# A two-layer adaLN kernel: its weights loaded in three groups with a semaphore each, its modulation and gate rows made inside the first image

## What is computed

```python
mod = (_silu(L0_c) @ L0_wmod).reshape(L0_c.shape[0], 6, 1, -1)
sa, ca, ga, sb, cb, gb = (mod[:, 0], mod[:, 1], mod[:, 2], mod[:, 3], mod[:, 4], mod[:, 5])
ga = (2 * (ga >= 0) - 1) * jnp.maximum(jnp.abs(ga), 0.25)
gb = (2 * (gb >= 0) - 1) * jnp.maximum(jnp.abs(gb), 0.25)
h = _layernorm(x, axis=-1) * (1 + ca) + sa
x = x + ga * _L0_attn_ref(h, ...)      # selective scan mixer
h = _layernorm(x, axis=-1) * (1 + cb) + sb
x = x + gb * _L0_ffn_ref(h, ...)       # routed experts, 8 of width 64, and a shared one
# layer 1: the same wrapping around _L1_attn_ref (gated delta rule, 8 heads)
# and _L1_ffn_ref (attention and 8 experts of width 512)
```

## Time and profile before

| | |
|---|---|
| median of 3 runs | 2970.29 us (2969.28 to 2974.66) |
| the profiled execution | 2970.33 us |
| its span | 2968.5 us |
| TensorE / VectorE / ScalarE / GpSimd busy | 82% / 74% / 41% / 22% |
| transferred | 21.39 MB: 125 GB/s in the first of 40 equal slices of the span, 1 to 8 GB/s in the others |

### The profile page before, as it was taken

One profiled execution on the slowest core, in us unless ns is written; L12 is line 12 of the kernel. 1 busy time (PEld: TensorE's weight loads), 2 busy tenths in 40 slices (PEclk: granted clock), 3 DMA queues, 4 the chain that ended last, 5 costly groups with the idle time before them and its releaser, 6 DMA issues.

```text
span 2968.5 us, 60546 instructions
## 1 busy us (share of the span) xinstructions
PE 2431.9 (82%) x22424; PEld 1916.4 (65%) x22424; DVE 2207.0 (74%) x5056; ACT 1202.5 (41%) x2697; POOL 650.6 (22%) x465
## 2 busy tenths in 40 slices
PE   1478878979887897978889887887988789798897
PEld 1166766757666585756757676675866667576685
DVE  1668777787977778787787877778697777878752
ACT  0333532435344253533525353343534425353432
POOL 0222122131212212122132212213121221312110
PEclk9569989989899998989989998998989899898999
DMA  4000000000000000000000000000000000000000
GB/s 125 2 2 3 1 7 3 7 3 7 2 3 7 3 7 3 1 8 2 8 3 7 2 3 7 3 7 3 7 2 3 7 3 7 3 3 5 1 6 2
DMA packets 24830, 21.39 MB, mean 7 GB/s; under 512 B 7217, under 2 KB 21570, under 8 KB 24530
## 3 DMA queue, kind: packets, MB, share of 16 engines
q1 hardware_dynamic: 24530, 17.26, 2.1%
HBM read 15.13 MB, written 2.13 MB: 6 GB/s over the span
## 4 chain that ended last, share of the span: by engine, by line
PE 42%; issue 27%; DVE 23%; POOL 5%; ACT 2%; SPq 1%; DMA 1%; DVEq 0%; POOLq 0%; ACTq 0%
PE banks L978 6%; PE banks L1151 4%; PE banks L1004 4%; PE banks L1141 4%; PE banks L855 4%; DVE wide L1336 3%; PE banks L970 3%; DVE wide L1324 3%; DVE wide L1344 2%; PE banks L996 2%; PE banks L918 2%; PE banks L960 2%; POOL lg L539 2%; DVE inv L1507 2%; PE banks L927 2%
## 5 line engine op out<-in xcount | busy, mean ns | idle before, releaser
L535 POOL TENSOR_TENSOR wide<-wide 128x512 f32<-128x512 f32 x128 | 260.2, 2033 | 861.0 <-DVE wide L1344 543.5
L1456 DVE SCALAR_TENSOR_TENSOR wide<-pad,conv,wide 128x256 f32<-128x256 f32 x864 | 368.6, 494 | 0.0
L637 ACT ACTIVATE wide<-small,a_neg 128x255 f32<-128x255 f32 x512 | 217.7, 496 | 188.0 <-DVE wide L1336 187.9
L1336 DVE TENSOR_TENSOR_SCAN wide<-wide 128x1024 f32<-128x1024 f32 x128 | 291.6, 2278 | 1.9 <-ACT wide L637 0.3
L762 ACT ACTIVATE inv<-banks,up1b 128x256 f32<-128x256 f32 x512 | 212.1, 489 | 126.6 <-PE banks L1141 126.4
L1141 PE MATMUL banks<-inv,up 128*128 128x256 f32 x1024 | 262.3, 387 | 0.0
L1151 PE MATMUL banks<-down,inv 128*128 128x128 f32 x2048 | 258.9, 277 | 0.0
L1151 PEld LDWEIGHTS banks<-down,inv 128*128 128x128 f32 x2048 | 248.7, 192 | 5.0
L832 PE MATMUL banks<-bc,sel3b 96*128 96x256 bf16 x512 | 110.4, 323 | 162.5 <-DVE wide L1344 134.3
L978 PE MATMUL banks<-inv 64*64 64x64 f32 x5120 | 200.9, 237 | 48.1 <-DVE inv L1507 44.3
L978 PEld LDWEIGHTS banks<-inv 64*64 64x64 f32 x5120 | 184.8, 151 | 73.7 <-issue 73.6
(11 more groups left out here) (277 smaller groups left out, 4966.3 us busy)
## 6 DMA issues: line engine op xcount, KB each, us to landing
gates_bc<-gate_rows SPq DMA_DIRECT2D x32, 128.0 KB, 2.9
up<-in_W SPq DMA_DIRECT2D x1, 2048.0 KB
x<-in_x SPq DMA_DIRECT2D x16, 128.0 KB, 2.2
out<-xn_y SPq DMA_DIRECT2D x16, 128.0 KB, 2.1
wide<-in_wmod SPq DMA_DIRECT2D x2, 384.0 KB
con<-in_con SPq DMA_DIRECT2D x1, 724.0 KB
w_k<-in_Wk SPq DMA_DIRECT2D x1, 512.0 KB
w_q<-in_Wq SPq DMA_DIRECT2D x1, 512.0 KB
```

The source lines that it names most:

```text
L535: g.tensor_tensor(ypart[p % 2], r[:, 0:512], r[:, 512:1024], ALU.add).then_inc(a_yp.h, 1)
L637: last = s.activation(decay[st % 2][:, at + 1:at + T], dt[:, c, 1:T], ACT.Exp, scale=a_neg[:, c, st * SG + q:st * SG + q + 1])
L1336: v.tensor_tensor_scan(state[st % 2], decay[st % 2], drive[st % 2], 0.0, ALU.mult, ALU.add).then_inc(a_h.h, 1)
L1456: v.scalar_tensor_tensor(dst, src, w, dst, ALU.mult, ALU.add).then_inc(c_conv.h, 1)
```

## The change

The list of loads is cut in three, each with a semaphore of its own, and its order is altered:
- `loads` (5): `c` of both layers, `con`, both parts of `wmod`. `load_x(0)` is issued after the first two of them.
- `loads_first` (12): what the first half reads up to the end of the scan, with `expA`, `norm_half` and `up0b` moved up to them.
- `loads_late` (26): the rest. `up1` and `down1` are now the last two.

The prologue's waits are for `loaded` (5 transfers) alone. ScalarE waits for `loaded_first` before L587, TensorE before the first transpose of image 0. `loaded_late` is waited for by ScalarE in `c_proj`, by TensorE in `a_out` and by VectorE in `a_res`, of image 0 alone.

VectorE's steps after silu(c) are no longer in the prologue. They are two functions, `modulation` (L1178 to L1182) and `gate_rows` (L1184 to L1202), which are called at the end of image 0's `a_norm2`, behind the normalised rows. Waits that go with this: ScalarE waits for `prep_dve` 8 (shifts and scales) where it waited for 12; TensorE and GpSimd wait for `prep_dve` no longer; GpSimd waits for `mod_done` before it writes zeros into `wide`, and for `prep_act` 7 only in `c_gate`; GpSimd's constants are filled ahead of its wait for `loaded`.

```diff
         loads = [
-            (con[:], a["con"]), (cT[:, 0, :], a["c0T"]), (cT[:, 1, :], a["c1T"]),
+            (cT[:, 0, :], a["c0T"]), (cT[:, 1, :], a["c1T"]), (con[:], a["con"]),
             (wmod[:, 0, :], a["wmod0"]), (wmod[:, 1, :], a["wmod1"]),
+        ]
+        loads_first = [
             (w_in[:], a["w_inT"]),
...
+            (expA[:], a["A_log1"].partition_broadcast(P)),
+            (norm_half[:], a["norm_w"].partition_broadcast(P)),
+            (up0b[:], a["up0b"]),
+        ]
+        loads_late = [
             (w_out[:], a["w_outT"].rearrange("(c p) d -> p c d", p=P)),
...
+            (up1b[:], a["b1"]),
+            (down1b[:], a["b2"]),
             (up1[:], a["W1"].rearrange("e d f -> d e f")),
-            (up1b[:], a["b1"]),
             (down1[:], a["W2"].rearrange("e (m p) d -> p (e m) d", p=P)),
-            (down1b[:], a["b2"]),
         ]
@@ sync
-            for dst, src in loads:
+            for dst, src in loads[:2]:
                 sp_.dma_start(dst, src).then_inc(loaded, 16)
+            load_x(0)
+            for dst, src in loads[2:]:
+                sp_.dma_start(dst, src).then_inc(loaded, 16)
+            for dst, src in loads_first:
+                sp_.dma_start(dst, src).then_inc(loaded_first, 16)
+            for dst, src in loads_late:
+                sp_.dma_start(dst, src).then_inc(loaded_late, 16)
             sp_.wait_ge(prep_dve, 12)
             sp_.dma_start(gates_dram, gates[:].rearrange("b n d -> b (n d)")).then_inc(gates_stored, 16)
             sp_.wait_ge(gates_stored, 16)
-            load_x(0)
             load_gates(0, 0, gx_loaded)
@@ gpsimd
-            g.wait_ge(loaded, LOADED)
             g.memset(ones_col[:], 1.0)
...
+            g.wait_ge(loaded, LOADED)
             g.tensor_copy(identb[:], ident)
...
             g.wait_ge(prep_pool, 1)
-            g.wait_ge(prep_dve, 12)
...
             def a_norm(i):
                 rstd(i, 0)
+                if isinstance(i, int):
+                    g.wait_ge(mod_done, 1)
...
             def c_gate(i):
+                if isinstance(i, int):
+                    g.wait_ge(prep_act, 7)
@@ scalar
+            s.wait_ge(loaded_first, LOADED_FIRST)
             s.activation(a_neg[:], a_neg[:], ACT.Exp).then_inc(prep_act, 1)
...
-            s.wait_ge(prep_dve, 12)
+            s.wait_ge(prep_dve, 8)
...
             def c_proj(i, m):
+                if m == 0 and isinstance(i, int):
+                    s.wait_ge(loaded_late, LOADED_LATE)
@@ tensor
-            t.wait_ge(prep_dve, 12)
-            t.wait_ge(prep_act, 7)
             t.wait_ge(prep_pool, 1)
+            t.wait_ge(loaded_first, LOADED_FIRST)
...
             def a_out_(i):
+                if isinstance(i, int):
+                    t.wait_ge(loaded_late, LOADED_LATE)
                 t.wait_ge(a_ys.h, a_ys.at(i, 2))
@@ vector
             v.tensor_tensor(cT[:], cT[:], ec, ALU.mult).then_inc(prep_dve, 1)
-            v.wait_ge(mod_done, 1)
...
+            v.wait_ge(prep_pool, 1)
+            def modulation():
+                v.wait_ge(mod_done, 1)
...
+            def gate_rows():
...
+            def a_norm2(i):
+                norm2(i, 0)
+                if isinstance(i, int):
+                    modulation()
+                    gate_rows()
...
             def a_res(i):
+                if isinstance(i, int):
+                    v.wait_ge(loaded_late, LOADED_LATE)
                 v.wait_ge(a_out.h, a_out.at(i, 1))
```

More of the change, by code:

```diff
@@ L324, in build @@
         gm = sb("gm", [P, 4])
-        loaded = sem("weights_loaded")
+        loaded = sem("modulation_loaded")
+        loaded_first = sem("first_half_loaded")
+        loaded_late = sem("late_weights_loaded")
         mod_done = sem("modulation_products")
@@ L1177, in _ @@
             v.tensor_tensor(cT[:], cT[:], ec, ALU.mult).then_inc(prep_dve, 1)
-            v.wait_ge(mod_done, 1)
-            v.tensor_copy(shift_scale[:].rearrange("p n b -> p (n b)"), bank(4, 8 * NB)).then_inc(prep_dve, 1)
-            v.wait_ge(prep_dve, 4)
-            for n in range(4):
-                v.tensor_scalar(shift_scale[:, 2 * n + 1, :], shift_scale[:, 2 * n + 1, :], 1.0, None, ALU.add).then_inc(prep_dve, 1)
-            g4 = PS[0:NB, 5, :]
-            sgn = inv[0:NB, 0]
-            mag = inv[0:NB, 1]
@@ L1196, in _ @@
-            v.wait_ge(silu_c, 5)
-            v.tensor_tensor(gates[:].rearrange("b n d -> b (n d)"), sgn, mag, ALU.mult).then_inc(prep_dve, 1)
-            v.wait_ge(prep_dve, 11)
-            v.tensor_scalar(gates[:, 0, :], gates[:, 0, :], 0.5, None, ALU.mult).then_inc(prep_dve, 1)
-            v.wait_ge(prep_dve, 12)
-            v.wait_ge(prep_act, 7)
-            v.wait_ge(prep_pool, 1)
+            v.wait_ge(prep_pool, 1)
+            def modulation():
+                v.wait_ge(mod_done, 1)
+                v.tensor_copy(shift_scale[:].rearrange("p n b -> p (n b)"), bank(4, 8 * NB)).then_inc(prep_dve, 1)
+                v.wait_ge(prep_dve, 4)
+                for n in range(4):
+                    v.tensor_scalar(shift_scale[:, 2 * n + 1, :], shift_scale[:, 2 * n + 1, :], 1.0, None, ALU.add).then_inc(prep_dve, 1)
@@ new lines, in gate_rows @@
+            def gate_rows():
+                g4 = PS[0:NB, 5, :]
+                sgn = inv[0:NB, 0]
+                mag = inv[0:NB, 1]
+                neg = inv[0:NB, 2]
+                v.tensor_scalar(sgn, g4, 0.0, 2.0, ALU.is_ge, ALU.mult).then_inc(prep_dve, 1)
+                v.tensor_scalar(mag, g4, -1.0, -0.25, ALU.mult, ALU.min).then_inc(prep_dve, 1)
+                v.wait_ge(prep_dve, 10)
+                v.tensor_scalar(neg, g4, -0.25, None, ALU.min).then_inc(silu_c, 1)
+                v.wait_ge(silu_c, 3)
+                v.tensor_tensor(mag, mag, neg, ALU.min).then_inc(silu_c, 1)
+                v.tensor_scalar(sgn, sgn, 1.0, -1.0, ALU.subtract, ALU.mult).then_inc(silu_c, 1)
+                v.wait_ge(silu_c, 5)
+                v.tensor_tensor(gates[:].rearrange("b n d -> b (n d)"), sgn, mag, ALU.mult).then_inc(prep_dve, 1)
+                v.wait_ge(prep_dve, 11)
+                v.tensor_scalar(gates[:, 0, :], gates[:, 0, :], 0.5, None, ALU.mult).then_inc(prep_dve, 1)
+                v.wait_ge(prep_dve, 12)
+                v.wait_ge(prep_act, 7)
@@ L1637, in d_res @@
                 residual(i, 3, yacc)
-            follow(v, TURNS["vector"], dict(a_norm=lambda i: norm(i, 0), a_norm2=lambda i: norm2(i, 0), a_conv=a_conv_, a_zgate=a_zgate,
+            follow(v, TURNS["vector"], dict(a_norm=lambda i: norm(i, 0), a_norm2=a_norm2, a_conv=a_conv_, a_zgate=a_zgate,
                            a_silu2=a_silu2, a_split=a_split_, a_soft=a_soft1, a_step=a_step, a_scan=a_scan, a_read=a_read, a_y=a_y_, a_res=a_res,
```

24 lines of the change are left out of this document (9 added, 15 removed).

## The result

The change takes 2921.05 us (median of 4 runs, 2917.40 to 2923.64), before took 2969.78 in the same comparison (4 runs, 2960.30 to 2974.66). The ratio is 0.9839, with an interval of 0.9812 to 0.9866. So it is faster, as forecast, but by 48.7 us and not by 40; the range (2925.5 to 2937) does not hold it. The profiled execution took 2920.56 us with a span of 2918.8.

A forecast was written before the change was run, and what follows sets the result against it. Bound at the start by waiting for the last weight, `down1b`, until 39.71 us, then a chain with little overlap. Gains of 29.5 (first group) and 10.7 us (to first tap) sum to 40.2, giving 2930 us, range 2925.5 to 2937.

The forecast's parts named there:

- rival 1: Whole kernel: the forecast itself, the first tap's shift arrives at the end, 2930 us; chance 0.72.
- The first group: Start of program: engines start at 10.2 us (bounds 8.3 to 12.2) instead of 39.71, a gain of 29.5 us.
- From there to the tap, 11.78 us: First group's completion to first tap: 11.78 us instead of 22.46, gain 10.7 us, VectorE's gate rows ending last.
- The second group: Twelve small loads before image 0's transposes: complete at 12 us, needed at 17.3, so they cost nothing.
- The late group and the gate rows: Remaining weights end near 39 us, gate rows land near 45, first used near 83; nothing waits.
- Work beside running transfers: Engines computing from 10 to 39 us while weights are written: no slowdown taken; a tenth longer would be 2.9 us.
- Rival 3: Program start: transfers slow the engines or a queue engine lags, first group at 12.2 us, total 2935 us; chance 0.09.
- TensorE's clock in image 0: Image 0's projections: a lifted clock would cut L817 and L819 from 3.7 to about 2.0 us; not in the forecast.
- rival 2: Image 0: TensorE's clock rises and holds until the projections, 1.7 us more gained, total 2928.3 us; chance 0.12.
- The groups complete apart: Weight loads: packet counts show the queue worked off nearly in issue order, so the first group completes before the whole list.
- rivals 4 and 5: Loads: groups do not complete apart, 2959.6 us, chance 0.03; loop: TensorE's branch back costs 50 us more, 2980, chance 0.04.
- The sum's base and the range's width: Whole kernel: base 2970.3 us; range from rivals' values, widened by one us below and two above for run spread.

The follow-up runs named there:

- change_again: The change itself, unedited, timed again against before: 2926.44 us (5 runs), ratio 0.9877.
- waits_only: The kernel before with only extra, long satisfied waits at the places where the change has its own: 2967.09 us (12 runs), ratio 1.0001.
- x_behind_weights: The change with the first image's rows of x issued behind all weights and not third: 2953.59 us (6 runs), ratio 0.9968.
- rows_behind_silu: The change with con after the first group, gate rows behind image 0's silu, four small loads issued from ScalarE's queue: 2924.37 us, ratio 0.9863.

## Why the prediction was wrong

The mechanism was the one forecast, rival 1: the first tap moved and the end moved with it. Two things in the numbers failed. In the gain, it was the term of the first group, 10.2 us where 8.82 were measured. In the time and its range, it was the base of 2970.3 us, which 44 runs put at 2965.95, and the 1 to 2 us allowed for the spread of runs, where the change's 13 runs spread over 20.6. The second is the larger; the gain's error alone would have left the time in the range. The steps came as follows.

- **The first group, "so 1.4 us more: 10.2 us".** This is the term of the gain that failed. It came at 8.82, within 0.5 us of the lower bound (8.3) and not at the value taken; in the other profiles with the same order of issue at 8.91, 9.01, 8.88 and 9.61, and at 8.57 without x ahead. I had let the whole delay of `con`'s issue through to the end. The packets in the traces say how the 1.4 us divide: the last 3 KB packet of `wmod` ends at 8.03 us in before, as I had it, and at 8.41 in the change, so the later issue cost 0.4 us and not 1.4; and ScalarE starts 0.41 us behind that packet, where I took 0.8 (behind the whole list of before it is 0.69: last packet at 39.02, start at 39.71). The views by windows suggest why the delay shrank: the transfers made up for it. Before, GB/s in the microseconds from 3, 4, 5 and 6 us, last column:

```profile
3.00:4.00 1.00, 0.00 (x0) 0.00 (x0) 0.00 (x0) 0.00 (x0) 0.00 (x0) 1.00 1.00 383
4.00:5.00 1.00, 0.00 (x0) 0.00 (x0) 0.00 (x0) 0.00 (x0) 0.00 (x0) 1.00 1.03 192
5.00:6.00 1.00, 0.00 (x0) 0.00 (x0) 0.00 (x0) 0.00 (x0) 0.00 (x0) 1.00 0.76 298
6.00:7.00 1.00, 0.00 (x0) 0.00 (x0) 0.00 (x0) 0.00 (x0) 0.00 (x0) 1.00 1.03 364
```

and in the change:

```profile
3.00:4.00 1.00, 0.00 (x0) 0.00 (x0) 0.00 (x0) 0.00 (x0) 0.00 (x0) 1.00 0.97 245
4.00:5.00 1.00, 0.00 (x0) 0.00 (x0) 0.00 (x0) 0.00 (x0) 0.00 (x0) 1.00 0.96 342
5.00:6.00 1.00, 0.00 (x0) 0.00 (x0) 0.00 (x0) 0.00 (x0) 0.00 (x0) 1.00 1.00 380
6.00:7.00 1.00, 0.00 (x0) 0.00 (x0) 0.00 (x0) 0.00 (x0) 0.00 (x0) 1.00 0.93 359
7.00:8.00 1.00, 0.00 (x0) 0.00 (x0) 0.00 (x0) 0.00 (x0) 0.00 (x0) 1.00 1.01 394
```

  By 7 us the change has moved 1.40 MB where before had 1.59, but with the small transfers of `c` out of the way and x's rows moved in the gap, 380, 359 and 394 GB/s followed where there had been 298 and 364. The term for the delay should have been nearer the bytes' 0.5 us. Size of both together: 1.4 us.
- **From there to the tap, 11.78 us.** 11.60 measured; the last gate row did end as the later of the two paths. Right, 0.2 us too long.
- **The second group.** Complete at 12.80, forecast 12; no wait on TensorE. Right.
- **The late group and the gate rows.** The end came near 42 us, not 39. SyncE was held up 6.16 us at `w_ba` where it had been 4.32, which goes with it; that it is the whole reason is not shown. Gate rows near 47 instead of 45, `a_res` at 83.35. Costs nothing, as forecast.
- **Work beside running transfers.** Nothing: the six taps from 21.07 us take 2.46 us together, as before without a transfer. Rival 3 falls.

```profile
62.82 2.46 DVE L1281 SCALAR_TENSOR_TENSOR small<-pad,conv,small 128x256 f32<-128x256 f32 x6
```
```profile
21.07 2.46 DVE L1315 SCALAR_TENSOR_TENSOR small<-pad,conv,small 128x256 f32<-128x256 f32 x6
...
25.63 2.02 PE L837 MATMUL banks<-small,w_bc 128*96 128x256 f32 x4 [4.58 <-DVE small L1320]
...
27.58 1.88 PE L839 MATMUL banks<-small,w_rank 128*8 128x256 f32 x4
```

- **TensorE's clock in image 0.** The projections L837 and L839 (L817 and L819 of before) took 2.02 and 1.88 us against 2.02 and 1.76. They stayed at the lower level though products, transposes and first projection now follow each other, so rival 2 falls. The clock did rise early in one execution, but it did not hold: the trace's record of the granted clock starts, at the upper level, at 20.7 us in change_again, just as `a_in` ends (L831, 18.93 to 20.84), and falls at 24.2, ahead of L837 at 25.41; in the change it starts at 30.0, behind L839, and L846 right after it runs at the upper level. The Trainium skill (TensorE: Matmul & The Clock Gate, "What's actually happening") has activity release the clock; here the 5.4 us of products and the `a_in` behind them did not do it in the one execution, and in the other for too short a time to show in the projections' durations. The measurement decides.
- **The groups complete apart**, and the loop's branch is unchanged: rivals 4 and 5 fall, the latter also by waits_only.

The shift was thus 41.75 us, forecast 40.2. **The sum's base and the range's width** are what took the time out of it. The base of 2970.3 was the median of three runs and of one profile; 44 runs of the same kernel give 2965.95, 4.4 us less. And I took the spread of runs for 1 to 2 us, though the three that I had spread over 5.4; the change's runs go from 2917.4 to 2938.0. The four runs behind the 2921.05 lie 3.4 us below the median of 13. From 2930 to 2921 are 9 us: 1.6 from the gain, 4.4 from the base and 3.4 that these four runs happened to be fast (medians do not add up exactly); the four runs of before in the same comparison lay 3.8 us above the median of 44, and with both the difference there was 48.7 us.

## What to carry to other kernels

A semaphore that counts a whole list of transfers makes the first instruction wait for the last byte; split it by first use, but then look for each thing that still stands at the end of the list or behind another queue's wait, since one 128 KB transfer at the end of the list cost 30 of 42 us. Price a change at the start of a program by when the first instruction of the untouched chain starts: one profile shows it to half a us, and over eight kernels the total followed it within 3 us. Take base and range of a forecast from the scatter of many runs, not from the median of three.

## What the runs showed of the hardware that was not expected

- Executions of one unchanged single-core program spread over 15 us (2959.7 to 2974.7 in 44 runs of before). Over the twelve profiles here TensorE's busy time in the loop differs by 10.9 us (2084.9 to 2095.8) and VectorE's by 0.9 (1923.9 to 1924.8). The tail's length goes with the granted clock, from 123.3 us at 0.94 to 127.5 at 0.90; the scatter of whole executions is explained by it in part.
- The issue of a transfer takes 0.43 us in most rows, but SyncE is held up when much is under way: 6.16 us at `w_ba`, behind the 2304 packets of 16 bytes of `conv1`; and behind the two 2 MB loads 9.92 us at `down1b` in before, 11.06 us at the store of the gate rows in the change and 10.90 us at x in x_behind_weights. What stands behind such an issue on its engine waits too. In the change that cost nothing, since the gate rows are first used at 83.35 us; in x_behind_weights what stood there was the first thing that VectorE waits for.
- The same instruction of the same program ran at either level. In the profiled execution of the change and in that of change_again, the third projection (L826 of before), timeline:

```profile
30.18 1.13 PE L846 MATMUL banks<-rank_sb,w_dt 128*128 128x256 f32 x4 [0.73 <-ACT rank_sb L637]
```
```profile
29.96 2.07 PE L846 MATMUL banks<-rank_sb,w_dt 128*128 128x256 f32 x4 [0.73 <-ACT rank_sb L637]
```

  1.13 and 2.07 us. The clock column reads 1.00 for the start of every profile, though L817 and L819 ran there in the time of the lower level: in before the record of the clock starts only at 70.8 us, and a column of 1.00 ahead of such a start is no evidence of the upper level. In the profile of rows_behind_silu it starts at 75.4 us, though the third projection had run in 2.08 us at 27.41, so that part of that execution's high mean clock, 0.915, is only this.
